# Moving the first layer's weight product of a graph network from the node stage to the edge stage

## The reference

```python
def _L0_gnn_ref(h, W, b, src, dst):
    m = h[src]
    agg = jax.ops.segment_sum(m, dst, num_segments=h.shape[0])
    out = jax.nn.relu(agg @ W.T + b)
    return out
...
x = _layernorm(x + _L0_gnn_ref(x, L0_gnn_W, L0_gnn_b, src, dst), axis=-1)
```

## Time and profile before

| | |
|---|---|
| Time, median of 3 runs | 6624.19 us (6605.84 to 6630.1) |
| Profiled execution, its own time | 6624.27 us |
| Its span | 6622.5 us |
| Busy share of the span | PE 78%, PE's weight loads 56%, DVE 65%, ACT 41%, POOL 61% |
| Edge stage of the first layer | 65.2 to 680.6 us |
| Node stage of the first layer | 709.0 to 1407.0 us |

### The profile page before, as it was taken

How to read it: one execution, slowest core, us unless ns; L and a number is a source line. 1 busy time by engine, 2 the same in 40 slices (tenths; PEclk the granted TensorE clock), 3 DMA queues, 4 the chain that set the end, 5 groups by cost and what they waited for, 6 DMA issues and landing times. The chain is left out here.

```text
span 6622.5 us, 108943 instructions
## 1 busy us (share of the span) xinstructions
PE 5189.9 (78%) x29030; PEld 3716.2 (56%) x29030; DVE 4327.9 (65%) x15755; ACT 2747.1 (41%) x6645; POOL 4019.6 (61%) x3613
## 2 busy tenths in 40 slices
PE   4777799868886666487868999969898967776798
PEld 3655577744555555433337888735555535555576
DVE  4554677733335555477757888869999955555698
ACT  0000355521111111266643555557777742222355
POOL 4666366666666888677765545315555555544699
PEclk9899899978888788799988999989999978888999
DMA  4555566634445666699974555434444423333476
GB/s 129 169 176 168 155 184 178 172 108 133 131 130 109 106 106 106 117 310 312 302 226 132 149 148 149 116 98 128 131 127 132 127 73 72 74 72 71 127 199 185
DMA packets 1159174, 966.37 MB, mean 146 GB/s; under 512 B 156342, under 2 KB 970882, under 8 KB 1158564
## 3 DMA queue, kind: packets, MB, share of 16 engines
q1 hardware_dynamic: 977956, 684.36, 34.4%
q0 software_dynamic: 158368, 210.14, 15.7%
q10 hardware_dynamic: 22240, 64.90, 2.6%
HBM read 485.30 MB, written 496.79 MB: 148 GB/s over the span
## 5 line engine op out<-in xcount | busy, mean ns | idle before, releaser
L526 POOL DMA_INDIRECT tgt_tab<-l_nodes_ext,rank_at x392 | 452.8, 1155 | 411.4 <-ACT l_nodes_ext L2328 308.6
L1563 POOL DMA_INDIRECT agg<-l_edges_b_rows,l_edges_b_at x392 | 608.6, 1552 | 135.5 <-issue 76.8
L1851 POOL DMA_INDIRECT l_edges_kv<-kv_tab,src_i x392 | 399.6, 1019 | 401.7 <-DVE l_edges_v_e L1872 292.9
L2526 POOL DMA_INDIRECT l_edges_proj<-proj_tab,src_i x392 | 381.8, 974 | 384.0 <-DVE l_edges_msg L2499 254.2
L526 POOL DMA_INDIRECT to_col<-l_nodes_col_s,rank_row x392 | 415.0, 1059 | 323.5 <-ACT l_nodes_col_s L1257 213.8
L968 POOL DMA_INDIRECT l_edges_fetched<-in_x,src_i x392 | 382.6, 976 | 218.9 <-DMA dst_i<-in_dst 111.6
L898 ACT COPY l_edges_rows<-l_edges_sums 128x264 f32<-128x264 f32 (+1 forms) x294 | 122.1, 450 | 944.6 <-DMA dst_i<-in_dst 462.3
L1321 POOL DMA_INDIRECT l_edges_a_at_row<-to_row,src_i x392 | 378.9, 967 | 218.3 <-issue 111.4
L526 POOL DMA_INDIRECT q_tab<-l_nodes_qkvs,rank_at x392 | 401.7, 1025 | 147.4 <-issue 110.7
L851 DVE TENSOR_SCALAR l_edges_hot<-columns,local_edge 128x128 f32<-128x128 f32 (+3 forms) x784 | 257.6, 380 | 295.3 <-DMA dst_i<-in_dst 285.5
L1733 PE MATMUL l_nodes_y<-w_qkvs,l_nodes_x_t 128*128 128x512 f32 x784 | 419.5, 617 | 0.0
(11 more groups left out here) (364 smaller groups left out, 14451.4 us busy)
## 6 DMA issues: line engine op xcount, KB each, us to landing
agg<-zeros ACTq DMA_DIRECT2D x98, 516.0 KB
l_nodes_xg<-x SPq DMA_DIRECT2D x196, 256.0 KB
kv_tab<-l_nodes_qkvs SPq DMA_DIRECT2D x98, 512.0 KB
agg<-l_edges_rows SPq DMA_DIRECT2D x98, 266.0 KB
l_nodes_ag<-agg SPq DMA_DIRECT2D x98, 266.0 KB
proj_tab<-l_nodes_ext SPq DMA_DIRECT2D x98, 264.0 KB
l_nodes_ag<-agg SPq DMA_DIRECT2D x98, 258.0 KB
l_nodes_ag_odd<-agg SPq DMA_DIRECT2D x98, 258.0 KB
```

What stands on the lines that cost most here:

```text
L526: pool.indirect_dma_start(table, bass.IndirectOffsetOnAxis(ranks[:, n * G + j:n * G + j + 1].bitcast(U32), 0), rows[:, j, :], None, bounds ...
L1563: pool.indirect_dma_start(agg1[j // 2], bass.IndirectOffsetOnAxis(at[k][:, j:j + 1].bitcast(U32), 0), rows[k][:, j, :], None, compute_op=A ...
L1851: pool.indirect_dma_start(kv[k][:, j, :], None, kv_tab, bass.IndirectOffsetOnAxis(src_i[:, n * G + j:n * G + j + 1].bitcast(U32), 0),).the ...
L2526: pool.indirect_dma_start(proj[k][:, j, :], None, proj_tab, bass.IndirectOffsetOnAxis(src_i[:, n * G + j:n * G + j + 1].bitcast(U32), 0),) ...
```

## The change

There are four parts.

1. The edge stage makes the product with `w0_t` itself, on the sums by rank. `total_across` replaces `total`: four wide products (512, 384, 256 and 128 columns), with the gathered rows as the stationary side, give the sums with the features on partitions. ACT copies them to SBUF (`take_across`), and a round later `turn_across` (lag 3) multiplies by `w0_t`, which brings them back to one rank for each partition, and adds the carried row. `hot` and `fetched` are free at the new signal `hot_read`, at the end of `total_across`; `carried` at `summed`, at the end of `turn_across`.
2. The node stage spreads finished rows: ten 128x128 products straight into `y` (L511 in the changed kernel). The copy `copy_a` and the product `project` are gone, and the later steps' lags are one less.
3. The 37 DMAs of weights are issued behind those of the index lists, in the stage that loads the constants.
4. The 16 DMAs of masks go from SP in `edge_ranks` to ACT's queue at the start of the edge stage.

```diff
                     @block.sync
                     def _(sp):
                         sp.dma_start(dst_i[:], dst).then_inc(loaded[0], 16)
                         sp.dma_start(src_i[:], src).then_inc(loaded[1], 16)
+                        begin_weights(sp, zero_made)
                         for s in loaded:
                             sp.wait_ge(s, 16)
...
-                        if last_of is not None:
-                            sp.wait_ge(masked, 1)
-                            for table, mask in ((reset_tab, reset_s), (open_tab, open_s)):
-                                for h in range(H2):
-                                    sp.dma_start(table[:, h, :], mask[:]).then_inc(mask_out, 16)
-                            sp.wait_ge(mask_out, 2 * H2 * 16)
...
+            hot_read = summed
+            if through is not None:
+                across = [sb(f"across{k}", [P, GE]) for k in range(2)]
+                across_p = [ps(f"across_p{k}", [P, GE]) for k in range(2)]
+                hot_read, taken = sem("hot_read"), sem("taken")
...
                 if follows(i, k, 2):
-                    dve.wait_ge(summed, n - 1)
+                    dve.wait_ge(hot_read, n - 1)
...
+                if through is not None and follows(i, k, 2):
+                    dve.wait_ge(summed, n - 1)
...
+            def total_across(pe, i, k, messages):
+                n = place(i, k)
+                pe.wait_ge(marked, n + 1)
+                if follows(i, k, 2):
+                    pe.wait_ge(taken, n - 1)
+                for j in reversed(range(G)):
+                    last = pe.matmul(across_p[k % 2][:, 0:(j + 1) * P], messages[:, j, :], hot[k % 2][j][:], start=(j == G - 1), stop=(j == 0),
+                                     skip_group_check=True)
+                last.then_inc(hot_read, 1)
+            def take_across(act, i, k):
+                n = place(i, k)
+                act.wait_ge(hot_read, n + 1)
+                if follows(i, k, 2):
+                    act.wait_ge(summed, n - 1)
+                act.copy(across[k % 2][:], across_p[k % 2][:]).then_inc(taken, 1)
+            def turn_across(pe, i, k):
+                n = place(i, k)
+                pe.wait_ge(taken, n + 1)
+                if follows(i, k, 2):
+                    pe.wait_ge(evacuated, n - 1)
+                for t in reversed(range(G)):
+                    last = pe.matmul(sums[k % 2][0][:, t, :], across[k % 2][:, t * P:(t + 1) * P], through[:], start=True, stop=True)
+                if n:
+                    pe.wait_ge(evacuated, n)
+                    for t in range(G):
+                        last = pe.matmul(sums[k % 2][0][0:1, 0, :], carried[k % 2][:, t:t + 1], rows[(k - 1) % RING][:, t, 0:width],
+                                         start=False, stop=(t == G - 1), skip_group_check=True)
+                last.then_inc(summed, 1)
...
-                mark, mark_carry, total, empty, store, settle, summed, _ = compact_steps(space, agg0, D)
+                mark, mark_carry, (total_across, take_across, turn_across), empty, store, settle, fetched_read, _ = compact_steps(
+                    space, agg0, D, through=w0_t)
...
                             if reuses(i):
-                                pool.wait_ge(summed, n - RING + 1)
+                                pool.wait_ge(fetched_read, n - RING + 1)
...
                             for j in range(G):
                                 pe.wait_ge(gathered[k][j], i * 16 + 16)
-                            total(pe, i, k, fetched[k])
+                            total_across(pe, i, k, fetched[k])
...
-                        rotation(pe, groups, (2, gather_total), (0, tally), loop=False)
+                        rotation(pe, groups, (2, gather_total), (0, tally), (3, lambda i, k: turn_across(pe, i, k)), loop=False)
...
-                        rotation(act, groups, (0, lambda i, k: empty(act, i, k)), (0, clear), loop=False)
-                        act.wait_ge(cleared, 16 * (2 * pairs + 2))
+                        for table, mask in ((reset_tab, reset_s), (open_tab, open_s)):
+                            for h in range(H2):
+                                act.dma_start(table[:, h, :], mask[:]).then_inc(cleared, 16)
+                        rotation(act, groups, (1, lambda i, k: empty(act, i, k)), (0, lambda i, k: take_across(act, i, k)), (0, clear), loop=False)
+                        act.wait_ge(cleared, 16 * (2 * pairs + 2 + 2 * H2))
...
+        def begin_weights(sp, cleared):
+            for to, frm in plain:
+                sp.dma_start(to, frm).then_inc(weights_in, 16)
+            with nc.allow_non_contiguous_dma(reason="short columns, once"):
+                for to, name in short:
+                    sp.dma_start(to[:], column(name)).then_inc(weights_in, 16)
+                sp.wait_ge(cleared, 2)
+                for m, name in enumerate(("L3_gnn_a_src", "L3_gnn_a_tgt")):
+                    for h in range(H3):
+                        sp.dma_start(attend[h * C3:(h + 1) * C3, m * H3 + h:m * H3 + h + 1],
+                                     w[name][0, h, :].rearrange("(c a) -> c a", a=1)).then_inc(attend_in, 16)
...
                             n = place(i, k)
                             pe.wait_ge(window_in[k], i * 16 + 16)
                             pe.wait_ge(hot_made, n + 1)
-                            if follows(i, k, 1):
-                                pe.wait_ge(a_copied, n)
-                            for t in range(G):
-                                last = pe.matmul(spread_a[:, t * P:], ag[k][:, t, :], hot[k % 2][t][:], start=(t == 0), stop=(t == G - 1),
-                                                 skip_group_check=True)
-                            last.then_inc(a_spread, 1)
-                        def project(i, k):
-                            n = place(i, k)
-                            pe.wait_ge(a_copied, n + 1)
                             if follows(i, k, 2):
                                 pe.wait_ge(biased, n - 1)
-                            for j in range(G):
-                                last = pe.matmul(y[k % 2][:, j, :], ag_t[k][:, j * P:(j + 1) * P], w0_t[:], start=True, stop=True)
-                            last.then_inc(y_done, 1)
+                            spread_rows(pe, lambda j: y[k % 2][:, j, :], hot[k % 2], ag[k], D).then_inc(y_done, 1)
...
-                        rotation(pe, groups, (0, lambda i, k: spread_line(pe, i, k)), (2, spread), (8, turn_x1), (3, project), (9, project_x1), loop=False)
+                        rotation(pe, groups, (0, lambda i, k: spread_line(pe, i, k)), (2, spread), (7, turn_x1), (8, project_x1), loop=False)
...
-                        rotation(dve, groups, (1, lambda i, k: mark_line(dve, i, k, a_spread)), (6, lambda i, k: balance(dve, i, k)),
-                                 (10, row), (4, mix), loop=False)
+                        rotation(dve, groups, (1, lambda i, k: mark_line(dve, i, k, y_done)), (5, lambda i, k: balance(dve, i, k)),
+                                 (9, row), (3, mix), loop=False)
...
                     def _(act):
-                        def copy_a(i, k):
-                            n = place(i, k)
-                            act.wait_ge(a_spread, n + 1)
-                            if reuses(i):
-                                act.wait_ge(y_done, n - RING + 1)
-                            act.copy(ag_t[k][:], spread_a[:]).then_inc(a_copied, 1)
...
-                        rotation(act, groups, (0, lambda i, k: copy_line(act, i, k)), (5, lambda i, k: root(act, i, k)), (2, copy_a), (8, copy_x1), (7, apply), (9, col), loop=False)
+                        rotation(act, groups, (0, lambda i, k: copy_line(act, i, k)), (4, lambda i, k: root(act, i, k)), (7, copy_x1), (6, apply), (8, col), loop=False)
```

89 lines of the change are left out of this document (38 added, 51 removed).

## The result

The changed kernel took **6776.35 us** (median of 4 runs, 6773.6 to 6783.87) against 6620.05 us for the kernel before (median of 4 runs, 6605.84 to 6630.1, one more than the table ahead of the prediction has): a ratio of **1.0241** (95% interval 1.0227 to 1.0256). The direction was forecast, the size was not: 6700 was said (76 us more than before), and 6776 (156 more) lies outside 6520 to 6750.

A forecast was written before the change was run, and what follows sets the result against it. It took PE signals seen late, only after POOL's indirect-DMA bursts, to lock edge and node stages. Sum: 6624.3 - 14.3 (start) + 91 (edge stage) + 0 (node stage) = 6701, said as 6700 us; 8-in-10 range 6520 to 6750.

The forecast's parts named there:

- The start: Program start: weights' DMAs behind the index loads let the edge stage begin at 50.9 instead of 65.3, -14.3 us.
- Here I expect the cost: Edge stage waits: PE's end of round, DVE's carried vector and PE's next start stand in series; +91 us.
- one round of PE for each release, one buffer freed, one group in the next burst: Edge stage loop: bursts of four gathers, 7.1 us for one group in place of 12.3 for two.
- rival (c): Edge stage: POOL lacks a free buffer at a release, 10.0 us a group, +370, about 6980; chance 0.05.
- wrong if gathers still come in eights: Edge stage sign: gathers were to come in fours; bursts of eight would show the forecast wrong.
- By work alone the edge stage would not become slower: Edge stage work: PE's round of about 4.9 us stays under POOL's four issues of 5.2.
- The node stage at nothing: Node stage: stays about 698 us, its loop of 13.46 for two groups unchanged; 0 in the sum.
- the bound below: Node stage: most it could gain, all of PE's 0.89 us for each of 98 groups, -87.
- The premise: Edge and node stages: PE's signals during a burst of indirect DMAs are seen only after its last one.
- Rival (b): Late signals follow PE's work, not the burst: node stage -87, edge stage stays 6.15 a group, 6523; chance 0.3.
- rival (a): Edge stage keeps two groups for each burst, so only the start counts: 6610; chance 0.2.

The follow-up runs named there:

- e1_start: Kernel before with only the start changed (weights' DMAs behind index loads, masks' DMAs on ACT in the edge stage): 6035.47 us, ratio 0.9987.
- e4_carried4: Changed kernel with four buffers for the carried rank's vector in place of two: 5986.02 us, ratio 0.9906.
- e9_turn_first: Changed kernel, two carried buffers, with the weight product moved ahead of the wide products in PE's round: 5993.99 us, ratio 0.992.
- e5_after: Changed kernel, unaltered, run again in a session without late signals: 6031.58 us, ratio 0.9984.
- e2_nodes: Kernel before with start and node stage changed, edge stage as before, first layer's weight product left out: 5986.63 us, ratio 0.9911.
- e18_nodes: Kernel before with start and node stage changed, weight product left out, in a session with late signals: 6606.25 us, ratio 1.0041.
- e10_masks_sp: Changed kernel with four carried buffers and the sixteen mask DMAs on SP's queue in place of ACT's: 5990.12 us, ratio 0.9919.
- e3_edges: Kernel before with start and edge stage changed, node stage as before, weight product made twice: 6076.52 us, ratio 1.0063.

## Why the prediction was wrong

1. **The start** (-14.3): right, -13.4. The masks on ACT's queue cost nothing that can be seen. For the edge stage's 1280 columns the wide set and the narrow one both take 2.39 us (2.47 in 56 of the narrow sets of `e1_start`); in the node stage the ten narrow products take 2.50 against the wide set's 2.42. The Trainium skill's rule on larger matmuls ("Perfetto Trace Analysis", "Optimizing Tensor Performance", Matmuls) names no size; the 0.08 us that these sets differ by in the node stage goes its way, and is 8 us for 98 groups.
2. **"Here I expect the cost": DVE's `carried` between two rounds of PE.** The place was right: two different edits that undo it (`e4_carried4`, `e9_turn_first`) give back 38 and 36 us of the 41 where signals are in time, and with held and real late signals together four buffers gave back 136. Two things in it failed.
   - **The failed step is the shape of the loop:** "one round of PE for each release, one buffer freed, one group in the next burst", 7.1 us for a group. PE went on for two rounds after a release, because 33 of 98 copies came over 0.5 us late, one in each loop of twelve, and not every one that fell into a burst; POOL used up all four permissions and had none at the next release. That is the mechanism of rival (c), "at a release POOL has no free buffer and waits for the `hot_read` of the round that has just begun", with three groups for each loop where I had given it one and 10.0 us. The loops of twelve took 7.73 us for a group. Were all loops so, the stage would have lost (7.73 - 6.15) x 96 = 152; half of the groups went in shorter loops, and 116 was measured. That 91 lies near 116 is in part luck, since the loop behind it did not come. The sign given beforehand, "wrong if gathers still come in eights", had come as well: 15 bursts of eight.
   - "By work alone the edge stage would not become slower" left the hand-over out. A round of 4.9 us of work and 0.74 from PE's end over DVE to PE's next start (407.64 to 408.38 in `e5_after`) is 5.64, more than POOL's 5.2, with no burst under way. This alone is the 41 us of the sessions without late signals.
3. **The clock** was no term of the sum. After 5 to 6 us of rest the wide products ran at or near the lower of the two levels (granted clock 0.58 and 0.51 of full speed over the sets at 416.21 and 439.03), 4.1 to 4.6 us instead of 2.39, and POOL waited for their end: some 2 us of a loop of 23, 35 at most in the sixteen loops of twelve. In the whole stage 29 of 98 sets took over 3 us. What the stage would take at the full clock was not tried. The mean granted clock of the edge stage fell from 0.90 to 0.88, of the node stage from 0.96 to 0.88.
4. **The node stage at nothing** ("the loop of 13.46 for two groups holds PE for two rounds"). This is the larger miss in kind: the bound below was -87 and there was none above. Where signals are in time the stage gains 44 of the 87 (`e2_nodes`); where they are late it loses 43 (`e18_nodes`), with the same instructions. What failed is the tacit step that the late signal stays that of the scatter's own product, 1.5 us ahead of the scatter. In 24 of 42 loops it is that of the transpose, with L230 between, and the scatter comes 3.5 us behind the release. ACT's chain from L1269 to L1276 has no pause in it, so PE's lower clock adds nothing to these 2 us. Why the transpose's signal is now the late one was not tried: PE's round is 0.89 us shorter, its steps stand one lag closer, and its clock is more often low.
5. **The premise.** The prediction took "signals that PE raises while a burst of indirect DMAs runs are seen only when the burst's last one is through" for a property of the kernel, from one profile. The late signals come and go between sessions, and where they come not every signal within a burst is late (404.82 above). Rival (b), faster, had -87 for the node stage, and 44 of it came in the sessions without late signals; but its mechanism was another, and there the changed kernel is within 0.2% of the one before, since edge and node stage nearly cancel (+41, -44). And a sum in rival (a) is off: 91, 87 and 14 give 6614, not 6618, which changes nothing.

The shortest times of those tried are the changed kernel with four buffers, 5986.02 against 6041.18 for the kernel before in the same session (6031.58 for the changed kernel against 6041.44 in another), 0.9% less, and `e9_turn_first` and `e10_masks_sp` lie within 0.2% of it. All this is where signals are in time. Under late signals four buffers ran only together with held ones (1.0114), and whether they beat the kernel before there is open.

## What to carry to other kernels

When a step is split in two over engines, look at what each half's buffers are freed by: a small vector that shares a wait with the last product of a round puts an engine in series between two rounds, and one more buffer, or the product moved ahead in the round, takes it out. In a loop with a ring of permissions, count how many rounds the producer still gets before its permissions are gone, and ask whether the permission it then lacks is already on its way or begins only at the release. When a wait ends late, look at what stands behind the waiting instruction on its own engine: which of two signals is late made 2 us of difference in the node stage. And before a sum is built on a wait that no dependency explains, ask for a second profile of the same kernel.

## What the runs showed of the hardware that was not expected

In some sessions waits for a signal of PE end late while POOL issues indirect DMAs. In the edge stage of the kernel before, 50 of ACT's 98 copies of the sums start more than 0.5 us behind the end of the product that they wait for, most of them 3 to 7 us (once 13.0), and most at 2.4 to 2.9 us behind the start of a burst's last gather. In the changed kernel it is 33 of 98, 5.6 us at most. ACT and DVE go on at the same instant, POOL 0.8 us later. In `e1_start`, `e3_edges`, `e4_carried4`, `e5_after` and `e9_turn_first` none starts more than 0.04 us behind.

The same program then takes 6572 to 6620 or 6037 to 6041 us. For the changed kernel the spans are 6776.3 (first profile) and 6033.2 (`e5_after`), and 693 of the 743 us between them lie in four stages with indirect DMAs: the first layer's edge stage (734.8 against 557.7 from barrier to barrier), its node stage (750.4 and 570.0), the second layer's first edge stage (615.8 and 515.0) and the fourth layer's edge stage (781.6 and 547.0). The stages without indirect DMAs take the same to 0.2 us. It isn't fixed to one chip: one chip had sessions of both kinds. What causes it stays open.

In the loops of twelve of the changed edge stage the granted clock was at or near the lower of its two levels, 1.2 GHz of 2.4, behind PE's rest of 5 to 6 us, while with gaps of 0.5 to 0.7 us (`e5_after`) the stage's mean was 1.00.
